# A token mixer, a state-space block and a routed expert layer on one core: the third routed part moved ahead of all dense steps

## The chip, the core and the metric

One NeuronCore of a Trainium2 chip runs the kernel in one launch. The metric is the device time of a run in microseconds; shown is the median of three runs. TensorE is called PE below, VectorE DVE, ScalarE ACT, GpSimd POOL and SyncE SP.

## What is computed

The input is `x` of 4 x 1024 tokens with 64 features. Three stages follow each other:

```python
h = prelu(((d_gamma * (q @ k.T)) @ v) @ Wo + bo)          # q, k, v = x @ W + b; 1024 x 1024 scores
h = h + ssm(layernorm(h))                                 # a scan over time, 128 channels
h = h + ffn(layernorm(h))                                 # 16 experts, the best 2 of each token

logits = x @ gate_w + gate_b
top_probs, top_idx = top_k(softmax(logits), 2)            # dispatch: 16 weights a token, 14 are zero
hidden = silu(x @ w1[e]) * (x @ w2[e])                    # 64 -> 128
out = sum over e of (hidden @ w3[e]) * dispatch[e]        # 128 -> 64
```

## The kernel before, in words

**Units.** The tokens are cut into four units of 1024 tokens: two batches ("halves") by two stretches of 512 time steps. The first two stages run over the units in `BEATS`, and the experts' work of the first units is laid into the late beats (`expert_pieces_at`).

**Two ways through the experts.** Units 0 to 2 are *routed* (`ROUTED_UNITS`): POOL scatters every token's row twice into a DRAM array `slots`, sorted by expert in blocks of 128 rows (`scatter`), the experts run on these blocks, and POOL gathers the two results of each token back (`gather`); DVE then weighs and adds them (`combine`). A part, that is one routed unit, has 8 groups of 4 blocks. The first four groups take each expert's own block, the last four take the blocks that are left over, with weights that are looked up at run time and loaded one block at a time (`load_weights`, `w12_shared`). Unit 3 is *dense*: all its tokens go through all 16 experts, the inputs of `w2` being weighed with the token's dispatch weight first (`weigh`), and the sum stays in PSUM. That is 32 steps, 16 experts for each half of the unit's columns. The dispatch weights are turned, stored to a DRAM array `given` of 16 rows per batch (`store_given`), and then loaded with each row spread over 64 partitions (`spread_given`, line L461, eight loads of 512 KB into the tensor `dg`, four experts and one batch each).

**The order.** `ITEMS` is the list of all 24 routed groups and 32 dense steps; `DENSE_RUNS` says how many dense steps stand ahead of part 0, 1 and 2 and at the end. Two items make a pair, and the pair's number is `i`: there are 28 pairs, 0 to 27. Before the change pairs 0 to 7 are the groups of parts 0 and 1, pairs 8 to 11 are 8 dense steps, pairs 12 to 15 are part 2, pairs 16 to 27 are 24 dense steps. Each engine runs `expert_piece(i, piece)` for pieces 0 to 3 of every pair in turn. On PE, pieces 0 and 1 are the pair's two hidden products (`hidden` L971, `hidden_dense` L1013), piece 2 the results of the pair before (`result` L988, `result_dense` L1025), and piece 3 `turn_slots(i + 2)` (L934), which transposes the 1024 rows that the routed pair two places on will use. On DVE, pieces 0 and 1 weigh the two experts that the next pair takes, in its first 16 dense steps (L1296), piece 1 also holds a `combine` (L1323 to L1325) where `COMBINE_AFTER` names the pair, and pieces 2 and 3 the two products `gated` (L1283). ACT computes silu (L681), takes the turned rows (L675) and stores routed results (L687, L690).

**SP's queue.** SP issues the loads in one fixed order. `load_slots(n)` (L470) brings the 1024 rows of the n-th routed pair, 256 KB, into one of `SLOT_BUFS` = 2 buffers, and so waits until `turn_slots(n - 2)` has left it. Behind `load_slots(n)` stand those `load_weights(k)` (L485, four loads of 64 KB) for which `WEIGHTS_AFTER[k]` is n, the store of the dispatch weights for `GIVEN_AFTER` = n, and all eight spread loads for `SPREAD_AFTER` = n:

```python
for n in range(ROUTED // 2):
    load_slots(n)
    if n == GIVEN_AFTER:
        store_given()
    if n == SPREAD_AFTER:
        for i in range(GIVEN_LOADS):
            spread_given(i)
```

The dispatch weights are turned by PE in pairs 4 to 6 (`X_PAIR`, `GIVEN_PAIRS`), before and after the change alike. POOL's order is three scatters, then three gathers.

Of the kernel before, what the change touches and what calls it, by code (L numbers as in the profile page):

```python
# [90 lines left out]
SLOT_BUFS = 2  # L91
ACT_BUFS = 4

WEIGHTS_AFTER = (-2, -2, -2, -2, -1, 3, 3, 6, 7, 7, 9, 11)

GIVEN_AFTER = 9
SPREAD_AFTER = 9

X_PAIR = 4
GIVEN_PAIRS = (5, 6)  # L100
# [10 lines left out]


LEAD = 2
DENSE_RUNS = (0, 0, 8, 24)

FIRST_TURN = 18

# [1 line left out]
def items():  # L119
    order, e = [], 0  # L120
    for r, n in enumerate(DENSE_RUNS):
        order += [("dense", k) for k in range(e, e + n)]
# [6 lines left out]
ITEMS = items()  # L129
ROUTED_POS = [ITEMS.index(("routed", g)) for g in range(ROUTED)]  # L130
DENSE_POS = [ITEMS.index(("dense", k)) for k in range(DENSE)]
COMBINE_AFTER = (13, 14, 20, 22, 24, 27)
WARM = 50
WARM2 = 20

# [51 lines left out]
def out_order():  # L187
    order = []
    routed = [(u, m) for u in ROUTED_UNITS for m in range(COMBINES)]
    for n in range(ALL_PAIRS + 2):  # L190
        order += [part for part, at in zip(routed, COMBINE_AFTER) if at == n]
        if n in ADD_AT:
# [7 lines left out]
def build_layer(nc, xT, dgT, wqk, vecs, wssm, wgate, rows, wvo, wy, w12, w3, out):  # L200
    with ExitStack() as ctx:
# [210 lines left out]
        def _(sp):  # L412
# [36 lines left out]
            def store_given():  # L449

                sp.wait_ge(given_done, BH)
                for b in range(BH):
                    sp.dma_start(given_dram[b], given_t[:, b, :]).then_inc(given_stored, 16)
# [20 lines left out]
            def load_weights(k):  # L474

                r, g = part_and_group(SHARED_AT[k])
                if g == OWN_GROUPS:
                    sp.wait_ge(owner_done, r + 1)
                _, owner = nc.values_load_multi_w_load_instructions(
                    owner_i[0:1, k * GB:(k + 1) * GB], engines=[SP_ENGINE], min_val=0, max_val=NE - 1,  # L480
                    skip_runtime_bounds_check_because="the owner of a block is at most NE - 1")
                if k >= WEIGHT_BUFS:
                    sp.wait_ge(hid_done, ROUTED_POS[SHARED_AT[k - WEIGHT_BUFS]] + 1)
                for j in range(GB):
                    sp.dma_start(w12_shared[rows_b(j % 2), k % WEIGHT_BUFS, j // 2, :],  # L485
                                 w12[bass.ds(owner[j] * D, D), :]).then_inc(ld_shared[k % WEIGHT_BUFS], 16)


            for k in range(len(SHARED_NO)):
                if WEIGHTS_AFTER[k] < 0:  # L490
                    load_weights(k)
# [7 lines that stand above are left out]
                for k in range(len(SHARED_NO)):  # L499
                    if WEIGHTS_AFTER[k] == n:  # L500
                        load_weights(k)
# [615 lines left out]
        def _(dve):  # L1117
# [186 lines left out]
            def expert_piece(i, piece):  # L1304
# [5 lines left out]
                if piece == 1:  # L1310
                    for c, at in enumerate(COMBINE_AFTER):
                        if at == i:
# [124 lines left out]
```

## Time and profile before

| | |
|---|---|
| median of 3 runs | 258.87 us (258.83 to 259.51) |
| span of the profiled execution | 331.5 us |
| what lies around that span | not shown; the span is its own time here |
| span less median | 72.6 us |
| PE busy (matmuls) | 257.1 us, 78% |
| DVE busy | 160.1 us, 48% |
| ACT busy | 119.7 us, 36% |
| POOL busy | 98.2 us, 30% |
| moved by DMA | 29.74 MB, mean 90 GB/s |
| mean granted clock of TensorE | 0.846 |

The profiled execution is 72.6 us longer than a run that is only timed, which is far more than the spread of the runs. So a stretch of the profile can't be read as a stretch of the run: some of its idle time is the profile's own, and has to be told from the kernel's. The lines of the profile name engine, line and tile; L470 and the like are lines of the kernel.

### The profile page before, as it was taken

The numbers are of one execution on the slowest core, as the hardware profiler recorded it, in microseconds if no ns is written. First come the engines' busy times: TensorE is split into PE (matmuls) and PEld (weight loads), VectorE is DVE, ScalarE is ACT, GpSimd is POOL, SyncE is SP. The second block draws the span as 40 slices with busy tenths as digits, with TensorE's granted clock in tenths as the row PEclk, the third lists the DMA queues.
The fourth block names the chain that finished last, engine by engine and source line by source line (L and its number), as shares of the span: only waits on it lengthen the run. The fifth ranks groups of instructions, "written<-read, shape, count | busy, mean of one in ns | idle before, by whom it ended". The sixth has DMA issues, their size and how long they took to land.

```text
span 331.5 us, 4678 instructions
## 1 busy us (share of the span) xinstructions
PE 257.1 (78%) x1645; PEld 156.7 (47%) x1645; DVE 160.1 (48%) x283; ACT 119.7 (36%) x283; POOL 98.2 (30%) x119
## 2 busy tenths in 40 slices
PE   8999999988935976258829995169964899952995
PEld 7443332532411323136529884168642698621563
DVE  1453649789805993167705610053410466710664
ACT  1302561764108711467534541022320344311341
POOL 4000000004760077303771047600476000674000
PEclk9999999999985999658965997555796599995699
DMA  7999800000111101332221675995121323021101
GB/s 191 371 388 278 170 0 0 4 0 12 40 51 57 33 20 52 89 95 73 55 58 44 154 160 131 209 222 114 41 59 28 83 65 78 19 44 20 34 16 32
DMA packets 45990, 29.74 MB, mean 90 GB/s; under 512 B 32688, under 2 KB 41072, under 8 KB 45456
## 3 DMA queue, kind: packets, MB, share of 16 engines
q1 hardware_dynamic: 30416, 23.15, 27.1%
q10 hardware_dynamic: 12480, 3.15, 4.3%
q0 software_dynamic: 3072, 3.15, 3.9%
q8 instruction: 13, 0.21, 0.3%
q14 instruction: 9, 0.07, 0.1%
HBM read 20.46 MB, written 8.98 MB: 89 GB/s over the span
## 4 chain that ended last, share of the span: by engine, by line
PE 52%; another core or an unknown queue 19%; ACT 11%; DVE 10%; issue 7%; ACTq 0%; POOL 0%; DVEq 0%; POOLq 0%
PE ring L1013 10%; PE ring L971 9%; PE turn L988 7%; PE side L1025 5%; PE acc L816 4%; PE ring L802 4%; ACT squares L611 3%; PE side L843 3%; DVE mixed L1141 2%; PE ring L759 2%; PE side L775 2%; ACT n L629 2%; PE acc L934 1%; DVE state L1190 1%
## 5 line engine op out<-in xcount | busy, mean ns | idle before, releaser
L559 POOL DMA_INDIRECT slots<-n,slot_i x48 | 47.8, 996 | 121.9 <-DVE slot_i L1256 108.2
L1283 DVE TENSOR_TENSOR act<-ring,silu 128x512 f32<-128x512 f32 x56 | 38.4, 690 | 89.5 <-ACT silu L681 68.6
L569 POOL DMA_INDIRECT back_v<-results,slot_i x48 | 46.5, 968 | 81.4 <-DMA results<-res 67.7
L681 ACT ACTIVATE silu<-ring 128x512 f32<-128x512 f32 x56 | 33.3, 597 | 78.7 <-remote 38.5
L1141 DVE TENSOR_TENSOR mixed<-ring,dg 128x1024 f32<-128x1024 f32 x32 | 38.6, 1218 | 19.5 <-remote 10.9
L816 PE MATMUL acc<-mixed,v 128*64 128x512 f32 x128 | 34.3, 628 | 8.6 <-DVE mixed L1141 8.4
L802 PE MATMUL ring<-kq 64*128 64x512 f32 x128 | 33.5, 629 | 0.0
L1013 PE MATMUL ring<-nT,w_sb 64*128 64x256 f32 x128 | 24.2, 459 | 8.8 <-issue 8.0
L971 PE MATMUL ring<-slots_t,w_shared 64*128 64x128 f32 x192 | 19.8, 328 | 13.7 <-issue 12.7
L988 PE MATMUL turn<-w_sb,act 128*128 128x64 f32 (+1 forms) x192 | 29.1, 314 | 0.0
L988 PEld LDWEIGHTS turn<-w_sb,act 128*128 128x128 f32 x192 | 27.3, 226 | 3.0 <-issue 2.2
L971 PEld LDWEIGHTS ring<-slots_t,w_shared 64*128 64x128 f32 x192 | 16.7, 229 | 17.2 <-issue 17.1
L971 PE MATMUL ring<-slots_t,w_sb 64*128 64x128 f32 x192 | 18.3, 314 | 8.1 <-issue 7.9
L843 PE MATMUL side<-nT,wssm_sb 64*128 64x512 f32 x64 | 19.0, 673 | 3.8 <-DVE drive L1175 2.7
L1025 PE MATMUL side<-act,w_sb 128*64 128x256 f32 x128 | 19.6, 432 | 3.0 <-ACT sum_t L665 2.2
L1013 PE MATMUL ring<-dg,w_sb 64*128 64x256 f32 x128 | 21.9, 424 | 0.0
L971 PEld LDWEIGHTS ring<-slots_t,w_sb 64*128 64x128 f32 x192 | 15.4, 219 | 13.0 <-issue 12.7
L816 PEld LDWEIGHTS acc<-mixed,v 128*64 128x64 f32 x128 | 6.9, 137 | 28.3 <-DVE mixed L1141 17.1
L1013 PEld LDWEIGHTS ring<-nT,w_sb 64*128 64x128 f32 x128 | 12.4, 214 | 15.9 <-issue 10.8
L802 PEld LDWEIGHTS ring<-kq 64*128 64x128 f32 x128 | 11.3, 190 | 15.9 <-issue 13.5
L934 PE MATMUL acc<-ident,slots 128*128 128x128 f32 x48 | 9.4, 329 | 11.1 <-DMA slots<-slots 5.6
L595 ACT ACTIVATE hT<-acc,vec 128x512 f32<-128x512 f32 x4 | 2.7, 687 | 35.3 <-PE acc L816 25.3
(150 smaller groups left out, 306.5 us busy)
## 6 DMA issues: line engine op xcount, KB each, us to landing
dg<-dgT SPq DMA_DIRECT2D x8, 512.0 KB, 7.8
dg<-given SPq DMA_DIRECT2D x8, 512.0 KB, 15.7
slots<-zeros SPq DMA_DIRECT2D x3, 1024.0 KB, 13.2
w_shared<-w SPq DMA_DIRECT2D x48, 64.0 KB, 2.2
slots<-slots SPq DMA_DIRECT2D x12, 256.0 KB
results<-res ACTq DMA_DIRECT2D x12, 256.0 KB, 2.9
w_sb<-w SPq DMA_DIRECT2D x2, 1024.0 KB, 14.3
xs<-xT SPq DMA_DIRECT2D x4, 256.0 KB, 6.5
```

The source lines that it names most:

```text
L559: pool.indirect_dma_start(out=slots_dram[r], out_offset=bass.IndirectOffsetOnAxis(ap=slot_i[:, r, k, i:i + 1], axis=0), in_=n2[:, u % 2, i ...
L569: pool.indirect_dma_start(out=back_v[:, r, i, k, :], out_offset=None, in_=results_dram[r], in_offset=bass.IndirectOffsetOnAxis(ap=slot_i[: ...
L681: s.activation(silu[:, n % 2], hidden_banks(n)[:, :, 0:PAIRS * P], ACT.Silu).then_inc(silu_done, 1)
L802: mm = pe.matmul(ring[:, 2 * (step % 2) + b, :], kq[rows_b(b), hh, 0, j * P:(j + 1) * P], kq[rows_b(b), hh, 1, th * CW:(th + 1) * CW], sta ...
L816: mm = pe.matmul(acc[rows_b(b), :], v[:, u // 2, j, b, :], mixed[:, step % MIX_BUFS, b, :], start=j == 0, stop=j == JT - 1)
L843: mm = pe.matmul(side[:, b, :], wssm_sb[rows_b(b), col:col + CH], nT[rows_b(b), :], start=True, stop=True)
L971: mm = pe.matmul(hidden_banks(p)[:, b, c:c + P], w[:, part * HID:(part + 1) * HID], slots_t[rows_b(b), n // 2 % 2, n % 2 * PAIRS + q, :], ...
L988: mm = pe.matmul(result_bank[:, (n % 2 * GB + k) * D:(n % 2 * GB + k + 1) * D], act[:, p % ACT_BUFS, k % 2, k // 2 * P:(k // 2 + 1) * P], ...
L1013: mm = pe.matmul(hidden_banks(p)[:, b, part * PAIRS * P:(part + 1) * PAIRS * P], w12_sb[rows_b(b), e, part * HID:(part + 1) * HID], x, sta ...
L1025: mm = pe.matmul(sum_bank[rows_b(b), :], w3_sb[:, e * D:(e + 1) * D], act[:, p % ACT_BUFS, b, :], start=e == 0, stop=e == NE - 1)
L1141: dve.tensor_tensor(mixed[:, step % MIX_BUFS], ring[:, r:r + 2, :], dg[:, u % 2, j, :].unsqueeze(1).broadcast_to([P, BH, CW]), ALU.mult).t ...
L1283: dve.tensor_tensor(act[:, n % ACT_BUFS], hidden_banks(n)[:, :, PAIRS * P:2 * PAIRS * P], silu[:, n % 2], ALU.mult).then_inc(act_done, 1)
```

## The change

It is made in four tables of numbers. The groups of part 2 follow those of part 1 without a gap (pairs 8 to 11), and all 32 dense steps come behind them (pairs 12 to 27). In SP's queue the shared weights of part 2's last two groups stand behind the ninth load of rows, and the spread loads behind the eleventh rather than the tenth. The combines move.

```diff
-WEIGHTS_AFTER = (-2, -2, -2, -2, -1, 3, 3, 6, 7, 7, 9, 11)
+WEIGHTS_AFTER = (-2, -2, -2, -2, -1, 3, 3, 6, 7, 7, 8, 8)
...
-SPREAD_AFTER = 9
+SPREAD_AFTER = 10
...
-DENSE_RUNS = (0, 0, 8, 24)
+DENSE_RUNS = (0, 0, 0, 32)
...
-COMBINE_AFTER = (13, 14, 20, 22, 24, 27)
+COMBINE_AFTER = (12, 13, 15, 18, 22, 25)
```

**SP's queue, the last loads of rows.** `slots` are rows, `given` the dispatch weights, `dg` what they are spread into, `w_shared` a shared block's weights. Before, from `load_slots(8)` on:

```order
L470 DMA slots<-slots 128x8x64 x2
L453 DMA given<-mixed 16x512 x2
L461 DMA dg<-given 64x2048 x8
L479 TENSOR_LOAD owner_i
L485 ISA
L485 DMA w_shared<-w 64x256
```

Now, from the last of the shared weights on:

```order
L485 DMA w_shared<-w 64x256
L470 DMA slots<-slots 128x8x64
L453 DMA given<-mixed 16x512 x2
L470 DMA slots<-slots 128x8x64
L461 DMA dg<-given 64x2048 x8
L470 DMA slots<-slots 128x8x64
L506 DMA out<-h 128x2x64 x16
```

Before, the eight spread loads went ahead of the rows of pairs 10 and 11 of the routed work, which stood behind 8 dense steps; now `load_slots(10)` is ahead of them and `load_slots(11)` directly behind.

**PE, pairs 8 to 10 of the change.** `acc<-ident,slots` is `turn_slots`, which needs its rows landed. The rows below begin with `turn_slots(10)` in pair 8, and the second L934 is `turn_slots(11)` in pair 9:

```order
L934 MATMUL acc<-ident,slots 128x128 x4
L971 MATMUL ring<-slots_t,w_sb 128x128 x16
L988 MATMUL turn<-w_sb,act 128x64 x8
L934 MATMUL acc<-ident,slots 128x128 x4
L957 TENSOR_LOAD owner_i
L971 MATMUL ring<-slots_t,w_shared 128x128 x8
```

`turn_slots(11)` stood in pair 13 before, four pairs later in the list; everything behind it on PE, the hidden products of pair 10 first, stands behind its wait.

**DVE, pairs 11 to 13 of the change.** L1283 is `gated`, L1296 `weigh`, L1323 to L1325 a `combine`:

```order
L1283 TENSOR_TENSOR act<-ring,silu 128x512 x2
L1296 TENSOR_TENSOR dg<-dg,nT 128x512 x2
L1323 TENSOR_TENSOR back_v<-back_v,weight 128x512
L1324 TENSOR_TENSOR h<-h,back_v 128x256
L1325 TENSOR_TENSOR h<-h,back_v 128x256
L1283 TENSOR_TENSOR act<-ring,silu 128x512 x2
```

Before, the pairs that weigh (7 to 10 and 15 to 18) and those that combine (13, 14, 20, 22, 24, 27) had none in common; now the weighing pairs are 11 to 18, and four of the six combines (12, 13, 15, 18) fall among them.

## Rows read from the trace of the kernel before

**Rows 1.** The page: the span, and the DMA rate in 40 slices of 8.3 us.

```profile
span 331.5 us, 4678 instructions
...
GB/s 191 371 388 278 170 0 0 4 0 12 40 51 57 33 20 52 89 95 73 55 58 44 154 160 131 209 222 114 41 59 28 83 65 78 19 44 20 34 16 32
```

**Rows 2.** Waits of ACT with no known releaser: us in total, times, longest.

```profile
ACT silu L681 <- remote: 38.5, 8, 16.9
...
ACT n L618 <- remote: 18.1, 3, 10.1
...
ACT slots_t L675 <- remote: 9.3, 1, 9.3
...
ACT sum_t L665 <- remote: 3.7, 1, 3.7
```

**Rows 3.** Timeline around pairs 6 to 8: start, length, engine, line, tiles.

```profile
198.42 2.08 PE L988 MATMUL turn<-w_sb,act 128*128 128x64 f32 x16
...
202.87 5.37 SPq L461 DMA_DIRECT2D dg<-given  x8
...
218.87 1.28 DVE L1296 TENSOR_TENSOR dg<-dg,nT 128x512 f32<-128x512 f32 x2
```

**Rows 4.** Stretches of 2 us: length, then PEclk, DMA share, GB/s.

```profile
204.00:206.00 2.00, 0.50 1.05 250
...
226.00:228.00 2.00, 0.50 0.98 221
228.00:230.00 2.00, 0.50 0.03 8
```

**Rows 5.** Tile `dg`, 195 to 262 us: the spread loads, and landing after issue.

```profile
L461 SPq DMA_DIRECT2D dg<-given x8: 5/578/713, 202.9 to 207.5; - x8
...
DMA to landing us min/median/max: 13.2/15.7/18.3
```

**Rows 6.** Tile `w_shared`: loads issued behind the spread loads; the page's median.

```profile
L485 SPq DMA_DIRECT2D w_shared<-w x4: 3/584/737, 211.1 to 217.7; - x4
...
DMA to landing us min/median/max: 8.9/10.3/14.9
...
w_shared<-w SPq DMA_DIRECT2D x48, 64.0 KB, 2.2
```

**Rows 7.** The chain in order of time: routed pair, half clock, dense pair.

```profile
187.21 1.09 PE ring L971 x16
188.30 1.93 PE turn L988 x16
190.23 0.45 PE acc L934 x4
...
232.10 3.71 PE ring L1013 x16
...
281.98 1.93 PE ring L1013 x16
283.90 1.01 PE side L1025 x8
```

**Rows 8.** Timeline of DVE in dense pairs: weighing, gating, a combine.

```profile
282.25 1.28 DVE L1296 TENSOR_TENSOR dg<-dg,nT 128x512 f32<-128x512 f32 x2
...
283.72 0.69 DVE L1283 TENSOR_TENSOR act<-ring,silu 128x512 f32<-128x512 f32 x1 [0.19 <-ACT silu L681]
...
288.13 0.68 DVE L1323 TENSOR_TENSOR back_v<-back_v,weight 128x512 f32<-128x512 f32 x1
...
288.85 0.42 DVE L1324 TENSOR_TENSOR h<-h,back_v 128x256 f32<-128x256 f32 x1
```

**Rows 9.** Stretches of 4 us: busy PE, PEld, DVE, ACT, POOL; PEclk, DMA, GB/s.

```profile
96.00:100.00 4.00, 0.00 (x0) 0.00 (x0) 0.00 (x0) 0.27 (x1) 1.92 (x2) 0.61 0.14 41
...
220.00:224.00 4.00, 4.00 (x26) 3.78 (x23) 2.65 (x5) 0.60 (x1) 0.00 (x0) 0.50 1.03 223
```

**Rows 10.** The page's DMA issues: a store of routed results, us to landing.

```profile
results<-res ACTq DMA_DIRECT2D x12, 256.0 KB, 2.9
```

## The prediction

> **What bounds the kernel now.** First the span against the times. The profiled execution took 331.5 us [rows 1] and the median run 258.87 us, so 72.6 us of the profile are not in a timed run. I looked for them among the waits: ACT has waits whose releaser the profile doesn't know, and their four largest entries are 38.5 + 18.1 + 9.3 + 3.7 = 69.6 us [rows 2]. That is nearly the whole difference. So I read the timeline with these waits taken out, and what is left of it as the timed run. The longest of them, 16.9 us [rows 2], lies right where this change is made, between the end of pair 6 and the first dense step: any true wait in that place is covered in this profile and has to be worked out.
>
> In the experts' work PE is the engine that sets the pace. The chain of waits runs along it in an even beat. A routed pair is two hidden products of 1.09 us, results of 1.93 and a transpose of 0.45 [rows 7], that is 4.56 us, and 4.11 without the transpose. A dense pair is 1.93 + 1.01 = 2.94 us [rows 7]. In such a pair DVE has two gatings and two weighings. A gating is read at 0.69 [rows 8], and the two weighings are 1.28 together [rows 8]: 2.66 of 2.94 us, so DVE is close behind. The clock matters too: with PE idle the granted clock fell from 1.00 to 0.50 (mean 0.61 over the stretch at 96 us [rows 9]), and at 220 us PE was busy throughout and still at 0.50 [rows 9], that is 1.2 instead of 2.4 GHz. A pair's hidden products then took 3.71 us [rows 7] where they take 1.93 at full clock.
>
> Then the DMA. The eight spread loads were issued from 202.87 us on [rows 3, 5], the last at 207.5, and that one landed 18.3 us later [rows 5], at 225.8. All that time the DMA engines were full: share 1.05 at 204 us, 0.98 at 226, 0.03 at 228 [rows 4]. 4.2 MB in about 21.5 us is 195 GB/s, and 221 GB/s is shown with the tail of it [rows 4], so 2.4 to 2.7 us a load. The shared weights that SP issued behind them, from 211.1 to 217.7, landed 14.9 us after issue at most and 8.9 at least [rows 6], that is between 226.0 and 226.6. Their usual landing is 2.2 us [rows 6]. So what stands behind the spread loads in SP's queue lands when these have drained, and not before. This is the reading on which the forecast rests.
>
> **The change, part by part.** The number of instructions stays the same on every engine, so the sum is one of waits.
>
> *Removed: the wait for the first spread loads.* Before, the results in piece 2 of pair 6 end at 200.4 [rows 3], pair 7 takes 2.18 + 1.93 = 4.1 us, and PE is ready for the first dense step at 204.5. It needs the first two loads and one weighing. From the landing of the last, 225.8, six loads back at 2.4 us give 211.4; from the start of the drain at about 204.3, two loads on at 2.7 give 209.7. I take 211.0 and 0.6 for the weighing: 211.6, a wait of 7.1 us. The lower bound is 5.8. The upper one is the first weighing as profiled, at 218.87 [rows 3], with 0.6 more: 15.0, since that weighing stood behind an unexplained wait on DVE's path and its data may have been there long before. I take 7.1 because the landings are nearer than a weighing held up by something else. After the change this load is needed in pair 11 and has some 10 us to spare. Gain: 7.1 us.
>
> *Added: the wait of the last rows.* `turn_slots(8)` comes back into pair 6, so pair 7 begins at 200.9. Pairs 7 and 8 take 4.56 each, and the first three pieces of pair 9 take 4.1: PE arrives at `turn_slots(11)` at 214.1. Its load stands directly behind the spread loads, whose order to `given`'s store is unchanged, so they are again issued at 202.9 to 207.5, and `load_slots(11)` at about 208.3. It can't land before 225.8. Its own 256 KB take from 1.2 us (at 221 GB/s [rows 4]) to 2.9 (a store of the same size and the same short rows [rows 10]), and I take 2.2. Three stores of results fall into the drain where one did before; two more of 0.26 MB at 221 GB/s [rows 4] are at most 2.4 us, at least nothing, and I take 1.0. So the rows are there at 229.0, and PE waits 14.9 us. Bounds: 12.9 and 17.0. Behind this wait on PE stand the hidden products of pair 10 and all that follows; ACT and DVE have nothing of their own to do meanwhile. Cost: 14.9 us.
>
> By the Trainium skill ("DMA: Bandwidth & Descriptors", Bandwidth) transfers of 1 MB ran at 341 GB/s; by that figure, an estimate, the drain would last 12.3 us and this wait would shrink to about 6, and the removed one to about 4. The trace differs: 221 GB/s with the engines full [rows 4], and the measurement decides.
>
> *Moved: combines among weighing pairs.* A combine is 0.68 and two additions of 0.42 [rows 8], with gaps 1.6 us. Alone it fits into a dense pair: 1.38 + 1.6 = 3.0. With a weighing it makes 4.3 us against 2.94 of PE. PE runs two steps ahead of the gating, which absorbs about 0.4 of the 1.3 us. Pairs 13, 15 and 18 so cost 1.0 each and pair 12, which has 3.9 us of PE, about 0.5: 3.5 us. Bounds: 0 (all absorbed) and 5.
>
> *At no cost.* The rows and shared weights of part 2 ahead of `store_given`: SP has from about 192 to 200.8 for them, and the two groups of shared weights take some 5 us of issue; were that cover gone, the store and the spread would be late by the rest. The third gather starts four pairs sooner; the combines at 22 and 25 leave it as much time as 24 and 27 did. The clock falls in either order, once, in the wait: after 7 us as after 15. What PE loses at half clock afterwards is up to some 8 us in both, and I set the difference to 0, with bounds of -4 and +5. The work of the last pairs is alike.
>
> *The sum.* 14.9 - 7.1 + 3.5 = +11.3 us. Against the profile's own 331.5 us that is 342.8, if the unexplained waits stayed as they are, which they need not. Against the median, 258.9 + 11.3 = 270.2; I say 270 us.
>
> **The rivals.**
>
> *The rows overtake the spread loads, and it is faster.* Place: `load_slots(11)`; it decides if these rows land before 214.1, that is within 5.8 us of their issue. Then PE never stops, 7.1 us are gained and 3.5 lost to DVE: 255.3 us. For it: 256 KB usually need about 2.9 us [rows 10]. Against it: four loads issued in the same place all landed at 226.0 or later [rows 6]. The Trainium skill ("DMA: Bandwidth & Descriptors", Two DMAs through the same engine are not ordered) says that a later DMA may complete before an earlier one; by that rule the rows could be early, and no row here shows such a case. Chance 0.12.
>
> *The wait before was as long as the profile's.* If the first dense step in truth began only at 218.9 + 0.6, the removed wait is 15.0 and the two cancel: 258.9 - 0.1 + 3.5 = 262.3 us. For it: the first weighing is at 218.87 [rows 3]. Against it: the landings. Chance 0.15. If DVE's overlap costs nothing besides, it is 258.8, no change: 0.06.
>
> *The spread loads are quicker in a timed run.* At the 388 GB/s of the third slice [rows 1] they drain in 10.8 us, by 215.1; the rows are there at 218.3 (4.2 us of wait), and the first dense step would have waited 3.1. That gives 258.9 + 4.2 - 3.1 + 3.5 = 263.5 us. Against it: share and rate under the drain [rows 4]. Chance 0.05.
>
> *The clock stays down for longer.* If PE comes back to full clock 14 us later than before, some 7 us are added: 277 us. Chance 0.06.
>
> **The numbers.** My forecast of 270 has the rest, 0.56; its own range is 265 to 276. The whole range, 261 to 277, takes in the second and the fourth rival and leaves out the faster case and the unchanged one, 0.18. Within 0.3% (0.8 us) a measurement of this kernel can hardly tell a change. Faster 0.12, same 0.06, slower 0.82.
>
> **What would show it.** Right: in the profile after, `load_slots(11)` lands with or behind the last spread load, PE is idle ahead of the second L934 behind the spread's issue, and no dense step waits for L1296. The gatings of pairs 13, 15 and 18 come late by one combine. Wrong: an L934 in pair 9 without a wait, a landing of a few us behind the spread loads, or the first dense pair before the change starting right behind a landing at 218 us.

## The result, and the profile after

| | before | after |
|---|---|---|
| median of the timed runs | 259.19 us (258.83 to 262.89, 4 runs) | 268.57 us (268.12 to 269.28, 4 runs) |
| ratio to before, 95% interval | | 1.038 (1.034 to 1.042) |
| profiled execution | 331.5 us span | 269.28 us, span 267.5 us |

The change makes the kernel 9.4 us slower. Medians here are of all runs; some executions of either kernel fall into a slower state (262.89 us among those of before), and the ratios leave these out. The forecast was 270.0 us, 1.4 us above the measured median, and its own range (265 to 276) held it.

The profile of before [rows 1] had 72.6 us in it that no timed run has. So the same kernel was profiled a second time (the first experiment below), and that profile, with a span of 257.5 us, is what the one of after is read against. The page of the changed kernel: span, busy time by engine, and the slices of the span for PE, its granted clock and the DMA.

```profile
span 267.5 us, 4678 instructions
...
PE 230.0 (86%) x1645; PEld 140.1 (52%) x1645; DVE 159.8 (60%) x283; ACT 119.3 (45%) x283; POOL 99.6 (37%) x119
...
PE   8999999999889989875888999998007998989994
PEclk9999999999999999997599999999556999999999
DMA  5999990000000231016423177799992362121100
```

PE is busy for as long as before, to 0.1 us (229.9 in the second profile of before). The loss is idle time in one place: the two slices with a 0, which begin 28 slices of 6.7 us into the span, at 187 us. The clock fell there too, and the DMA row reads 9 up to the same place (PE ends at 186.05 us). The stretches show it closer (length; busy PE, PEld, DVE, ACT, POOL; PEclk, DMA share, GB/s).

```profile
188.00:190.00 2.00, 0.00 (x0) 0.00 (x0) 0.00 (x0) 0.00 (x0) 0.00 (x0) 0.51 1.03 241
...
198.00:200.00 2.00, 0.00 (x0) 0.00 (x0) 0.00 (x0) 0.00 (x0) 0.00 (x0) 0.50 1.10 225
...
204.00:206.00 2.00, 2.00 (x28) 1.90 (x26) 0.13 (x1) 0.60 (x1) 1.39 (x3) 0.73 0.20 41
206.00:208.00 2.00, 2.00 (x20) 1.91 (x18) 1.79 (x4) 0.60 (x1) 1.69 (x2) 1.00 0.15 33
```

No engine computes anything from 188 to 200 us, and the DMA engines are full. When they empty, all starts again. [Rows 4] had the same share and rate, and no such stop was told apart in them, because that profile's unexplained waits lay over the place. Now who waited for what (total, times, longest, in us):

```profile
POOL back_v L569 <- DMA results<-res: 25.2, 2, 16.5
PE acc L934 <- DMA slots<-slots: 18.7, 2, 16.0
ACT res L687 <- DMA results<-res: 16.6, 1, 16.6
```

No wait has an unknown releaser here, as they had in [rows 2]. Three engines stopped, each on a DMA of its own: PE on the last rows, ACT on a store of results (L687 may write a result buffer only when the store from it has landed), POOL on the stores that its gather reads. The timeline gives the order (start, length, engine, line, tiles, and in brackets the wait before it):

```profile
176.17 5.81 SPq L461 DMA_DIRECT2D dg<-given  x8
...
178.00 0.39 ACTq L690 DMA_DIRECT2D results<-res  x1
...
182.02 0.59 SPq L470 DMA_DIRECT2D slots<-slots  x1
...
184.05 2.00 PE L988 MATMUL turn<-w_sb,act 128*128 128x64 f32 x16
...
201.39 0.60 ACT L687 ACTIVATE res<-turn 128x512 f32<-128x512 f32 x1 [16.62 <-DMA results<-res]
...
202.07 1.11 PE L934 MATMUL acc<-ident,slots 128*128 128x128 f32 x4 [16.02 <-DMA slots<-slots]
...
203.29 0.95 POOL L569 DMA_INDIRECT back_v<-results,slot_i  x1 [16.50 <-DMA results<-res]
```

PE had pair 9's results behind it at 186.05 and waited until 202.07 for rows issued at 182.02. The eight spread loads had been issued just ahead of them. The tile `dg` says when these landed:

```profile
L461 SPq DMA_DIRECT2D dg<-given x8: 467/588/1072, 176.2 to 181.4; - x8
...
DMA to landing us min/median/max: 6.4/13.6/19.3
```

The last of them, issued at 181.4, landed 19.3 us later, at 200.7. No dense step waits for L1296 any more.

The spread itself began later than before. SP's rows, first the changed kernel, then the kernel before in its second profile:

```profile
166.18 5.93 SPq L485 DMA_DIRECT2D w_shared<-w  x8
...
172.80 1.03 SPq L453 DMA_DIRECT2D given<-mixed  x2
```

```profile
170.36 1.61 SPq L453 DMA_DIRECT2D given<-mixed  x2
```

The eight loads of shared weights that now stand ahead of `store_given` hold SP until 172.1 us, so the store is issued 2.4 us later, and the first spread load too (176.17 against 173.79). PE is at the same point in both profiles at that time: it begins pair 7 at 173.35 and 172.66 us, apart by the one transpose that came back into pair 6.

### The profile page after: what moved, and what is told of

It reads as the page before. It is cut to its first block, busy times and chain, and to the rows that moved or that the text cites. A ratio compares the mean times of both kernels' runs of the same rounds, so it can differ in the third digit from the quotient of the medians.

```text
span 267.5 us, 4678 instructions
## 1 busy us (share of the span) xinstructions
PE 230.0 (86%) x1645; PEld 140.1 (52%) x1645; DVE 159.8 (60%) x283; ACT 119.3 (45%) x283; POOL 99.6 (37%) x119
## 4 chain that ended last, share of the span: by engine, by line
PE 51%; DVE 20%; ACT 9%; DMA 9%; issue 8%; SPq 1%; DVEq 0%; POOL 0%; ACTq 0%; POOLq 0%
DMA slots<-slots 9%; PE ring L1013 9%; PE ring L971 8%; PE turn L988 6%; PE ring L802 4%; PE side L1025 4%; PE acc L816 4%; ACT squares L611 3%; DVE mixed L1141 3%; PE side L843 3%; DVE state L1190 3%; PE ring L759 3%; PE side L775 2%; DVE dg L1296 2%; PE acc L934 2%
## 5 line engine op out<-in xcount | busy, mean ns | idle before, releaser
L1283 DVE TENSOR_TENSOR act<-ring,silu 128x512 f32<-128x512 f32 x56 | 38.0, 688 | 51.1 <-ACT silu L681 50.5
L569 POOL DMA_INDIRECT back_v<-results,slot_i x48 | 47.8, 995 | 39.2 <-DMA results<-res 25.2
L934 PE MATMUL acc<-ident,slots 128*128 128x128 f32 x48 | 8.8, 314 | 18.7 <-DMA slots<-slots 18.7
L988 PE MATMUL turn<-w_sb,act 128*128 128x64 f32 (+1 forms) x192 | 24.0, 278 | 0.0
L988 PEld LDWEIGHTS turn<-w_sb,act 128*128 128x128 f32 x192 | 22.3, 191 | 2.3 <-issue 1.1
L1013 PE MATMUL ring<-nT,w_sb 64*128 64x256 f32 x128 | 20.9, 401 | 2.0 <-DVE act L1283 1.9
L687 ACT ACTIVATE res<-turn 128x512 f32<-128x512 f32 x12 | 7.2, 597 | 29.2 <-DMA results<-res 16.6
L1013 PE MATMUL ring<-dg,w_sb 64*128 64x256 f32 x128 | 19.3, 376 | 0.0
L1025 PE MATMUL side<-act,w_sb 128*64 128x256 f32 x128 | 17.3, 392 | 0.0
L934 PEld LDWEIGHTS acc<-ident,slots 128*128 128x128 f32 x48 | 6.4, 169 | 19.3 <-DMA slots<-slots 16.2
L1013 PEld LDWEIGHTS ring<-nT,w_sb 64*128 64x128 f32 x128 | 11.3, 186 | 8.0 <-issue 4.6
L971 PE MATMUL ring<-slots_t,w_shared 64*128 64x128 f32 x192 | 13.8, 293 | 0.6 <-DVE act L1283 0.4
L971 PEld LDWEIGHTS ring<-slots_t,w_sb 64*128 64x128 f32 x192 | 12.6, 199 | 3.0 <-issue 2.5
## 6 DMA issues: line engine op xcount, KB each, us to landing
dg<-given SPq DMA_DIRECT2D x8, 512.0 KB, 13.6
```

Of the source, the lines that this page charges most:

```text
L569: pool.indirect_dma_start(out=back_v[:, r, i, k, :], out_offset=None, in_=results_dram[r], in_offset=bass.IndirectOffsetOnAxis(ap=slot_i[: ...
L971: mm = pe.matmul(hidden_banks(p)[:, b, c:c + P], w[:, part * HID:(part + 1) * HID], slots_t[rows_b(b), n // 2 % 2, n % 2 * PAIRS + q, :], ...
L988: mm = pe.matmul(result_bank[:, (n % 2 * GB + k) * D:(n % 2 * GB + k + 1) * D], act[:, p % ACT_BUFS, k % 2, k // 2 * P:(k // 2 + 1) * P], ...
L1013: mm = pe.matmul(hidden_banks(p)[:, b, part * PAIRS * P:(part + 1) * PAIRS * P], w12_sb[rows_b(b), e, part * HID:(part + 1) * HID], x, sta ...
L1025: mm = pe.matmul(sum_bank[rows_b(b), :], w3_sb[:, e * D:(e + 1) * D], act[:, p % ACT_BUFS, b, :], start=e == 0, stop=e == NE - 1)
L1283: dve.tensor_tensor(act[:, n % ACT_BUFS], hidden_banks(n)[:, :, PAIRS * P:2 * PAIRS * P], silu[:, n % 2], ALU.mult).then_inc(act_done, 1)
```

## The experiments

All changes are to the changed kernel unless it says otherwise. The kernel before was run again on each chip, beside the others; ratios are to those runs, with their 95% interval.

**The kernel before, profiled again.** No edit.

> The kernel before, unchanged, profiled once more, in the hope of a profile without the 69.6 us of unexplained waits on ACT. Theory (the forecast's): those waits are no part of a timed run, so this span, if free of them, is 256 to 259 us, and the one wait of its own between pair 6 and the first dense step is 6 to 9 us on PE, ending on DVE's first weighing (L1296). Rival (the wait was as long as in the first profile): 14 to 16 us there.

Measured 259.22 us, span 257.5. The timeline around the first dense step:

```profile
173.79 5.04 SPq L461 DMA_DIRECT2D dg<-given  x8
...
182.63 1.31 DVE L1296 TENSOR_TENSOR dg<-dg,nT 128x512 f32<-128x512 f32 x2 [10.46 <-DMA dg<-given]
...
184.69 1.22 PE L1013 MATMUL ring<-nT,w_sb 64*128 64x256 f32 x4 [8.05 <-DVE act L1283]
```

The span lies 1.7 us under the run's time, not 72.6: the unexplained waits belonged to the first profiled execution, not to the kernel. The removed wait is 8.05 us on PE (7.1 predicted), and the first weighing came 8.8 us after the first issue, so the 16 us between issue and first weighing in [rows 3] were a product of those waits. With that the rival "the wait before was as long as the profile's" falls. Here too the clock went to 0.50 in the wait and was back soon after PE (columns as in the stretches above):

```profile
182.00:184.00 2.00, 0.00 (x0) 0.00 (x0) 1.37 (x3) 0.00 (x0) 1.70 (x2) 0.50 1.01 202
...
188.00:190.00 2.00, 2.00 (x18) 1.86 (x16) 1.29 (x3) 0.60 (x1) 0.00 (x0) 1.00 0.91 204
```

Before, PE resumed at 184.7 and had a granted 1.00 from 188 us at the latest; after, it resumed at 202.1 and had it from 206 us at the latest, with a mean of 0.73 in the 2 us ahead. In stretches of 0.5 us the half clock ends at 187.7 and at 205.1: 3.0 us of busy PE at half clock in both of these profiles. That they agree is not a property of the two orders: in the profiles below PE, busy throughout, stayed at 0.50 for 3.5 to 8.7 us after such a wait, and no run shows what sets it.

**The last rows ahead of the spread loads.** This undoes the one thing the forecast rests on, the rows' place in SP's queue.

```diff
-SPREAD_AFTER = 10
+SPREAD_AFTER = 11
```

> The changed kernel with the spread loads behind the last load of rows (SPREAD_AFTER 11), nothing else. Theory A (the order in SP's queue alone made the wait of 16.0 us on PE): the rows land within 3 us, the wait goes, 251 to 254 us. Theory B (a second wall stands beside it: ACT waited 16.6 us in the same stretch for a store of results, in its own queue, that landed only when the spread loads had drained, and it has two result buffers): PE stops in pair 10 or 11 instead, 262 to 269 us.

Measured 265.27 us (264.52 to 265.87), ratio 1.027 (1.020 to 1.034); only 3.3 us of the 16 came back. PE's long wait for the rows is gone, but there is another, for ACT, which waits for a store (waits, then the timeline and the chain of waits, whose rows are start, length, who):

```profile
PE turn L988 <- ACT res L687: 11.2, 1, 11.2
```

```profile
181.24 0.37 ACTq L690 DMA_DIRECT2D results<-res  x1
...
201.75 0.60 ACT L687 ACTIVATE res<-turn 128x512 f32<-128x512 f32 x1 [13.75 <-DMA results<-res]
```

```profile
181.24 20.43 DMA results<-res
...
202.49 3.67 PE turn L988 x16
```

The store was issued at 181.24 and landed 20.4 us later, at the end of the drain, where such a store otherwise takes 2.9 [rows 10]. PE waits for ACT, and restarts at half clock as before (3.67 us where 1.93 is full clock [rows 7]), but stays there for longer, from 202.49 to 210.4 us (length; busy PE, PEld, DVE, ACT, POOL; PEclk, DMA share, GB/s):

```profile
208.00:210.00 2.00, 2.00 (x11) 1.18 (x8) 0.69 (x1) 0.68 (x2) 1.62 (x2) 0.50 0.93 196
```

So PE's wait fell by 4.8 us, from 16.0 to 11.2, and 7.9 us at half clock where the change had 3.0 took some 2.5 of them back (an estimate: half of the 4.9 us more). ACT's wait stood in the profile of after as well: it ended 0.7 us before PE's own and so cost nothing visible there. It is a second wall with nearly the same end.

**The same with four result buffers.** ACT then doesn't need that store before pair 11. The result buffers take the space of a tile that is free by then.

```diff
-SPREAD_AFTER = 10
+SPREAD_AFTER = 11
-RES_BUFS = 2
+RES_BUFS = 4
-        res = sb("res", [P, RES_BUFS, 2 * GB, D])
+        res = kq[:, 0, :, :].rearrange("p a (r n d) -> p (a r) n d", r=2, n=2 * GB)
```

> As the run before it, and with four result buffers instead of two (laid into the dead tensor kq), so that ACT need not wait for a store of the last two pairs. Theory A: as the run before it, 251 to 254 us. Theory B: the second wall goes too, and only here the time falls to 251 to 256 us; the stores still land at the end of the spread loads, 15 to 20 us after their issue.

Measured 262.35 us (261.73 to 262.87), ratio 1.016 (1.009 to 1.022). Another 2.9 us, above what either theory expected, and again less than the wait that was taken away. PE now waits twice, and the timeline shows for what:

```profile
189.89 7.44 ACTq L690 DMA_DIRECT2D results<-kq  x1
...
198.90 1.23 PE L1013 MATMUL ring<-nT,w_sb 64*128 64x256 f32 x4 [5.77 <-DVE act L1283]
...
202.26 0.94 POOL L569 DMA_INDIRECT back_v<-results,slot_i  x1 [16.56 <-DMA results<-kq]
...
214.90 0.69 DVE L1323 TENSOR_TENSOR back_v<-back_v,weight 128x512 f32<-128x512 f32 x1 [2.45 <-DMA back_v<-results,slot_i]
...
217.27 1.22 PE L1013 MATMUL ring<-nT,w_sb 64*128 64x256 f32 x4 [3.44 <-DVE act L1283]
```

The longer wait comes from ACT. The mere issue of a store at 189.89, under the drain, held ACT for 7.44 us, where such an issue otherwise takes 0.37; ACT's silu came at 197.44, the gating behind it, and PE had waited 5.77 us. The other is the gather's: POOL's second gather waited for a store until 202.26, the combine behind pair 15 waited for that gather, and PE waited 3.44 us for a gating that stood behind the combine on DVE. So there are four walls under the one drain: the rows, the store that ACT waits for, the issue of a store, and the gather. The first, second and fourth end with it, at 200 to 203 us.

**The combines away from the weighing pairs.** This measures the third term by itself.

```diff
-COMBINE_AFTER = (12, 13, 15, 18, 22, 25)
+COMBINE_AFTER = (19, 20, 21, 22, 24, 26)
```

> The changed kernel with the combines in pairs 19, 20, 21, 22, 24 and 26, none of them in a pair that weighs. The term of the sum: 3.5 us less, 265.1 us. As the profile after reads (pair 15 0.95 us, pair 18 0.95, pair 13 0.2, with pair 12 nothing): 2.1 us less, 266.5 us. If DVE's overlap costs nothing: 268.6 us.

Measured 266.84 us (265.32 to 269.50), ratio 1.037 (1.027 to 1.047): the times overlap with those of the change and tell nothing of a term of 0 to 3.5 us. The profiles do. In that of the change, PE waits for the gating behind the combines of pairs 15 and 18 (timeline):

```profile
225.76 0.70 PE L1013 MATMUL ring<-nT,w_sb 64*128 64x256 f32 x4 [0.93 <-DVE act L1283]
...
235.59 0.70 PE L1013 MATMUL ring<-nT,w_sb 64*128 64x256 f32 x4 [0.94 <-DVE act L1283]
```

That is 0.93 and 0.94 us. Pairs 12 to 15 begin at 211.86, 215.72, 218.88 and 221.82: pair 13 takes 3.16 us, 0.2 over the 2.94 of a dense pair, and pair 15 takes 3.94, 1.0 over. With the combines apart these waits are gone. The first dense step and the last results, of the change and then of this kernel:

```profile
211.86 0.70 PE L1013 MATMUL ring<-nT,w_sb 64*128 64x256 f32 x4
...
261.42 2.14 PE L1025 MATMUL side<-act,w_sb 128*64 128x256 f32 x16
```

```profile
210.12 0.70 PE L1013 MATMUL ring<-nT,w_sb 64*128 64x256 f32 x4
...
257.46 2.14 PE L1025 MATMUL side<-act,w_sb 128*64 128x256 f32 x16
```

The dense work takes 49.56 us and 47.34: the combines cost 2.2 us where the change has them. The runs' times hide this, because this profile also ran 2.7 us ahead already in pair 5, which the edit can't have caused, and stayed at half clock for 5.9 us after the wait and not 3.0.

**The spread loads over 128 partitions.** Four loads of twice the partitions instead of eight; `given` is stored in eight copies, so that each group of 16 partitions reads its own.

```diff
-        given_dram = nc.dram_tensor("given", [BH, NE, CW], F32).ap()
+        given_dram = nc.dram_tensor("given", [BH * COPIES, NE, CW], F32).ap()
...
-                for b in range(BH):
-                    sp.dma_start(weighed[rows_b(b), e, :], given_dram[b, e, :].unsqueeze(0).broadcast_to(...))
+                sp.dma_start(weighed[:, e, :], given_dram[:, e, :].unsqueeze(1).broadcast_to(...))
```

> The changed kernel with the same 4.2 MB spread by four loads that each write all 128 partitions, instead of eight that write 64 (the store of the dispatch weights writes 8 copies for it, 0.5 MB). Theory (eight loads of 64 partitions are slow because of how they write, 220 GB/s with the engines full, where other loads of this trace reach 388): the drain shrinks from 24 to 11 to 14 us, the rows behind it land some 10 us earlier, PE waits 3 to 8 us instead of 16.0: 256 to 261 us. Rival (they are slow because 64 partitions read the same 8 KB of DRAM): the drain and the time stay, 268 to 270 us.

Measured 273.33 us (272.98 to 273.69), ratio 1.059 (1.052 to 1.066). The timeline, the waits and one stretch in the drain:

```profile
180.40 3.41 SPq L462 DMA_DIRECT2D dg<-given  x4
```

```profile
PE acc L936 <- DMA slots<-slots: 20.8, 3, 16.7
```

```profile
196.00:200.00 4.00, 0.00 (x0) 0.00 (x0) 0.00 (x0) 0.00 (x0) 0.00 (x0) 0.50 1.02 244
```

The rate is 244 GB/s where it was 225 to 247 from 186 to 200 us; twice the partitions don't double it. The last rows came 24.9 us after the first spread issue (205.25), and 25.9 before. The spread began 4.2 us later, behind the larger store (180.40 instead of 176.17), and the kernel is slower by about that. The Trainium skill ("SBUF — State Buffer", Door 1: The DMA port swizzle) has 64 partitions reach only half of the ports; by that the drain should have been nearly halved (an estimate). It was not, so what limits this drain is something else. The same edit made to the kernel before, and to the version with four result buffers:

> The kernel before with the spread of 128 partitions. Its own wait for the first spread load was 8.05 us in the second profile. Theory: the first load of 1 MB lands in 4 to 6 us instead of 8.8, so 3 to 5 us less: 254 to 256 us. Rival (reading bounds it): 259 us.

> The changed kernel with the rows first, four result buffers and the spread of 128 partitions together. Theory (the spread loads are the only cause of the loss, through the rows, the stores and the third gather that waits for the stores): the waits are gone, 268.6 less 16 to 18 us: 250 to 253 us, below both kernels. Rival (another wait takes their place): 256 us or more.

They gave 264.29 us (261.10 to 266.89; the two that count for a comparison are 261.10 and 262.27, against 256.75 to 259.35 of the kernel before beside them) and 265.00 us (264.15 to 265.96), the latter with a ratio of 1.028 (1.020 to 1.036): both some 3 to 4 us slower than without the edit. The spread begins 3.5 and 3.7 us later in them (177.3 and 180.8 us), which is about what they lose; the rate brought nothing back. What holds it at 225 to 247 GB/s stays open.

**Rows first, and the spread in runs of 1 KB.** A spread load reads one run of 8 KB for each partition. Here each is cut in half by columns, which makes runs of 1 KB of the same bytes.

```diff
-SPREAD_AFTER = 10
+SPREAD_AFTER = 11
...
-                    sp.dma_start(weighed[rows_b(b), e, :], given_dram[b, e, :]...)
+                    for c in range(2):
+                        cols = slice(c * CW // 2, (c + 1) * CW // 2)
+                        sp.dma_start(weighed[rows_b(b), e, cols], given_dram[b, e, cols]...)
```

> As the run with the rows first (265.3 us), with the spread loads cut into 16 whose contiguous runs are 1 KB instead of 8 KB; the same bytes. Theory (each DMA engine takes a piece of one queue in turn with a piece of the other, so a store of 256 B rows gets one short row through per 8 KB run): the stores under the drain land within 5 to 12 us instead of 20, ACT's wait of 13.7 us goes, 252 to 257 us. Rival (the stores are late because the engines are full, whatever the pieces): no change, 264 to 267 us.

Measured 255.69 us (254.98 to 258.67), ratio 0.990 (0.983 to 0.996): 9.6 us less than with rows first alone, and below the kernel before. The timeline of ACT:

```profile
194.67 0.60 ACT L689 ACTIVATE res<-turn 128x512 f32<-128x512 f32 x1 [6.15 <-DMA results<-res]
```

ACT waits 6.15 us where it waited 13.75, and PE 3.6 us where it waited 11.2. That is 7.6 us; this profiled run, at 258.67 us the slowest of the five, stayed at half clock for 8.7 us behind the wait, and the others, with a higher granted clock, are 3 us shorter. Why the wait is shorter shows in the DMA queues (queue: packets, MB, share of 16 engines; q1 is SP's and q10 is ACT's here). First the changed kernel from 188 to 196 us, while the long runs were under way, then this one from 191 to 195 us:

```profile
q1 hardware_dynamic: 256, 1.66, 87.6%
...
q10 hardware_dynamic: 250, 0.06, 6.0%
```

```profile
q1 hardware_dynamic: 917, 0.88, 80.9%
q10 hardware_dynamic: 916, 0.23, 31.4%
```

In each case the two queues moved equally many packets (of SP's 256, 203 hold 8 KB), while SP's moved 27 times the bytes in the first and 4 times in the second. ACT's packets are the rows of a store, 256 bytes each; a store has 1024 of them, 64 for each DMA engine. 250 packets in 8 us are 16 for each engine, so 64 rows would take 33 us at this pace, longer than the drain: most of the store waits until the long runs are through. With runs of 1 KB it is 916 in 4 us, 57 for each engine, and 64 rows take 4.5 us. So the queues take turns by packets, whatever their size, and what a short transfer pays is the length of the other queue's packets. The Trainium skill ("DMA: Bandwidth & Descriptors", Queues, rings and completion order) has each DMA engine go round its queues packet by packet, with some 9 to 17 descriptors in a packet as typical. The equal counts, 256 and 250, agree with turns of equal number; how many rows go in one turn they can't tell.

The turns aren't all of it. The store of the change was issued at 178.00, and from 178 to 183 us ACT's queue moved no packet at all; here it was issued at 181.76, and from 182 to 187 us there was none either. These first 5 us are the same with long and short runs, and no run shows where they come from.

**Short runs in the order of the change.** Here the rows still stand behind the spread loads.

> The changed kernel, the last rows still behind the spread loads in SP's queue, these in runs of 1 KB. Theory (two causes: order within a queue, and turns between queues): the stores are quick, the rows still land only behind the last spread load, and since 16 issues take longer, at 195 to 199 us: PE waits 10 to 14 us in pair 9, 262 to 268 us. Rival (only the long runs cost): 254 to 258 us.

Measured 269.78 us (267.63 to 269.89), ratio 1.044 (1.034 to 1.055): no gain. Timeline:

```profile
190.84 1.17 SPq L472 DMA_DIRECT2D slots<-slots  x1
...
202.15 1.11 PE L936 MATMUL acc<-ident,slots 128*128 128x128 f32 x4 [17.57 <-DMA slots<-slots]
```

PE waited 17.6 us, more than the 10 to 14 expected. The sixteen issues took SP 14.5 us, so the rows were issued only at 190.84 and came at 202.15 with the end of the drain. Short runs don't help what stands behind them in their own queue. The stores were quick again: ACT waited for none, and POOL's gather began at 194.00 us where it had begun at 203.29.

**The last rows through ACT's queue.** In the order of the change, but `load_slots(11)` is issued by ACT in pair 7, while SP issues the first spread loads.

```diff
+                if piece == 3 and i == 7:
+                    s.wait_ge(scattered[PARTS - 1], 16 * 2 * UT)
+                    s.wait_ge(sturned, 10)
+                    s.dma_start(slots[:, 1, :, :], ...).then_inc(ld_slots[1], 16)
```

> The changed kernel with long runs, and the last rows loaded from ACT's queue instead of SP's, issued in pair 7. Theory (turns between queues, a short row against a run of 8 KB): leaving SP's queue helps little, the rows land 15 us or more after their issue, PE still waits 10 to 16 us, 264 to 270 us. Rival (the forecast's reading, the order in SP's queue alone): the rows land within 8 us and PE does not wait for them; the stores then set 262 to 267 us as in the run with the rows first.

Measured 266.20 us (265.46 to 267.98), ratio 1.035 (1.025 to 1.045). Timeline and waits:

```profile
175.27 0.37 ACTq L706 DMA_DIRECT2D slots<-slots  x1
```

```profile
PE acc L941 <- DMA slots<-slots: 17.2, 2, 14.8
...
ACT res L688 <- DMA results<-res: 13.8, 1, 13.8
```

Another queue doesn't save the rows: issued at 175.27, 2.1 us behind the first of the spread loads, they came at 198.2 (PE's next transpose, L941 here), 23 us later. PE's wait is only 1.2 us shorter than in the change, and by the interval this kernel is no faster. The rows are 1024 rows of 256 bytes like a store, and take turns with runs of 8 KB in the same way: from 182 to 195 us the two queues moved 380 and 381 packets.

**Short runs in the kernel before.**

> The kernel before with the spread loads in runs of 1 KB. Theory (its own wait is for the landing of the first quarter, which short runs don't speed up): the wait of about 8 us stays, 257 to 261 us, so what the run of short runs gained against this kernel comes from the order. Rival (short runs are quicker by themselves): 255 us or less.

Measured 259.72 us (255.98 to 263.07, 10 runs), ratio 1.001 (0.995 to 1.007). Its weighing still waits (timeline):

```profile
179.51 1.29 DVE L1298 TENSOR_TENSOR dg<-dg,nT 128x512 f32<-128x512 f32 x2 [9.65 <-DMA dg<-given]
```

There what is waited for is the spread itself, which short runs hardly bring sooner (9.65 us, and 10.46 with long ones). So the gain of short runs was seen only in an order whose walls are stores and gathers.

**All together.** Rows first, short runs, four result buffers, combines behind pairs 19 to 26.

> The changed order with the rows first, the spread loads in runs of 1 KB, four result buffers, and the combines in pairs 19 to 26 (none that weighs). Theory: it takes away what is left in the run of short runs (255.7 us): ACT's wait of 6.1 us for a store, the stretch at half clock behind it, and DVE's overlap of about 2 us; 248 to 252 us, below both kernels. Rival (another wait takes their place, the third gather at the end above all): 254 us or more.

Measured 249.39 us (247.20 to 255.59, 7 runs), ratio 0.964 (0.955 to 0.973). It beats both kernels: the order of the change, with what it collides with taken away.

## Why the prediction was right

The balance, between the profile of after (267.5 us) and the second one of before (257.5 us):

| term | predicted | measured |
|---|---|---|
| added: PE's wait for the last rows | +14.9 | +16.0 |
| removed: wait of the first dense step | -7.1 | -8.05 |
| combines among weighing pairs | +3.5 | +2.1 |
| clock | 0 | about 0 (3.0 us at half clock in both) |
| sum | +11.3 | +10.0 |

The spans differ by 10.0 us, the medians by 9.4. Place, cause and sign of the two large terms are as forecast. That the sum is right to 1.4 us is in part luck: errors of 1 to 2.4 us cancel, as follows.

*The profile's surplus.* To take the 69.6 us of unexplained waits out and forecast against the median was right: the second profile of the same kernel has none of them.

*The added wait.* The place, the cause and the sign are as forecast: the rows came 1.4 us after the last spread load's landing. PE arrived 9.9 us after the first spread issue, where the forecast had 11.2 (202.9 to 214.1); the rows came 25.9 after it, where it had 26.1. Both agreements hide errors. Under "at no cost" the forecast named the danger that the shared weights make the store and the spread late, and put it at nothing; they were 2.4 us late. Without that, an estimate from the two profiles, PE would have arrived 12.3 us behind the first issue and waited 13.6 us. And from the first issue to the last landing it took 24.5 us where the forecast had 22.9, while the rows came 1.4 us behind that landing and not 3.2.

*The removed wait* was read from the landings and not from the weighing in the profile, and that was the better witness: 8.05 against 7.1 and 15.0.

*The combines.* This term was sized too high. Pairs 15 and 18 cost 0.93 and 0.94 us, as forecast, pair 13 some 0.2 and not 1.0, pair 12 nothing and not 0.5. The three together are the 2.1 us of the table, and the kernel with the combines apart confirms them with 2.2. Of the sum it is the term that was furthest off in proportion, 1.4 us too high, and it hid what the added wait was too low by.

*The clock.* The forecast had up to some 8 us lost at half clock in both orders; 3.0 us at half clock lose 1.5. The difference of 0 came true, but by luck: other kernels stayed at half clock for up to 8.7 us after such a wait, which is 3 us more lost, and nothing in the forecast said which it would be here.

*The step that was wrong without showing.* "ACT and DVE have nothing of their own to do meanwhile", and the stores in the drain "are at most 2.4 us". The bytes were counted, and not the turns. A store issued at 178.00 held ACT until 201.39, and would have stopped PE to nearly the same time had the rows been there (with the rows first, PE restarts at 202.49 and not 202.07). So the forecast was right in its number, but its reading, that the place in SP's queue alone makes the wait, was only half of it: with the rows moved ahead, 3.3 of 16 us come back. With the rows in another queue the time is within the interval of the change itself.

*The rival "the rows overtake"* would have had PE run on. In no run did the last rows, where they stood behind the spread loads in SP's queue, come before these had drained. *The rival of quicker loads* falls with the rate of 225 to 247 GB/s under the drain.

*Shown and not shown.* Shown by edits: the place in the queue (rows first), the result buffers, the length of the runs, the queue, and in the profile the price of the combines. Argued from counts of packets, and borne out by the edit of the runs: that queues take turns by packets. Not settled: what limits the spread's rate, why another queue's first packet comes only some 5 us after its issue, why the issue of a store took 7.44 us, and what sets how long the clock stays down.

## What to carry to other kernels

A bulk load in long runs holds back every transfer of short rows until it has drained, in its own queue by order and in the others by turns; so put it behind the last urgent load, cut its runs short, and give what is stored meanwhile more buffers. When a wait is removed, look for the next one with nearly the same end: here three walls (rows, stores, gather) all ended with one drain and a fourth (the issue of a store) stood under it, and the first two fixes brought some 3 us each. What stands in an issuing engine's queue ahead of a bulk load delays it by its issue time: look what the engine does there before calling a move free. If a profiled span and the timed median differ by more than a few us, profile the kernel again; if it can't be done, find the unexplained waits first, and read waits in their place from landings.

## What the runs showed of the hardware that was not expected

- A store of 256 KB in rows of 256 bytes took up to 23 us beside loads in runs of 8 KB, 12.8 us at most beside the same bytes in runs of 1 KB (the kernel with rows first), and 2.9 us as the median of the kernel before [rows 10].
- Two queues moved equal numbers of packets, 256 and 250, though 203 of the one's held 8 KB and the other's hold 256 bytes each; the later queue's first packet came 5 us after its issue.
- The issue of one store under the full drain held ACT for 7.44 us.
- After waits of 3.6 to 16 us, a busy PE stayed at half clock for 3.0 us in two profiles and up to 8.7 us in others.
- Twice the partitions under a spread load left the rate at 244 GB/s (225 to 247 without).
- A profiled execution can carry 70 us of waits that a second one of the same kernel doesn't have.
